# Opening a projection phase with four interleaved value tiles, and wider buffering behind it, in a gated cross-attention block

## What is computed

```python
x = x + jnp.tanh(g_xattn[0]) * xattn(_layernorm(x), ctx, ctx, pos, mask, Wq, Wk, Wv, Wo)
x = x + jnp.tanh(g_ffn[0]) * ffn(_layernorm(x), gate_w, gate_b, w1, b1, w2, b2)
# xattn
q = (query @ Wq).reshape(nb, q_len, H, D).transpose(0, 2, 1, 3)
k = (key @ Wk).reshape(nb, q_len, KVH, D).transpose(0, 2, 1, 3)
v = (value @ Wv).reshape(nb, q_len, KVH, D).transpose(0, 2, 1, 3)
q = q * cos + _rotate_half(q) * sin
k = k * cos + _rotate_half(k) * sin
scores = jnp.einsum('bhqd,bhkd->bhqk', q, k) / jnp.sqrt(jnp.float32(D))
attn = jax.nn.softmax(jnp.where(mask == 0, -1e9, scores), axis=-1)
return jnp.einsum('bhqk,bhkd->bhqd', attn, v).transpose(0, 2, 1, 3).reshape(nb, q_len, H * D) @ Wo
```

## Time and profile before

| | |
|---|---|
| median of 3 runs | 736.51 us (736.07 to 739.14) |
| profiled execution, its own time | 737.81 us |
| its span, first to last instruction | 736.0 us |
| PE busy | 704.6 us, 96% |
| DVE busy | 558.4 us, 76% |
| POOL busy | 402.6 us, 55% |
| ACT busy | 357.0 us, 49% |
| granted TensorE clock, mean | 0.993 |
| moved by DMA | 71.10 MB, 97 GB/s |

### The profile page before, as it was taken

How to read it: one execution, slowest core, us unless ns; L and a number is a source line. 1 busy time by engine, 2 the same in 40 slices (tenths; PEclk the granted TensorE clock), 3 DMA queues, 4 the chain that set the end, 5 groups by cost and what they waited for, 6 DMA issues and landing times.

```text
span 736.0 us, 11337 instructions
## 1 busy us (share of the span) xinstructions
PE 704.6 (96%) x3478; PEld 587.7 (80%) x3478; DVE 558.4 (76%) x924; ACT 357.0 (49%) x955; POOL 402.6 (55%) x340
## 2 busy tenths in 40 slices
PE   5798899899999999999999999999999879999998
PEld 3686688688888888888888888888888766788886
DVE  4977778778878787878888887878787984378832
ACT  5522452455554545454545545454545574872130
POOL 5653524665766666666657566666666541383020
PEclk9999999999999999999999999999999999999999
DMA  8695465432133131212213112222222310240101
GB/s 285 223 288 204 171 216 185 129 101 64 52 87 87 58 87 57 82 61 72 71 36 109 58 56 86 86 57 87 58 77 67 104 69 29 58 115 14 58 1 58
DMA packets 66111, 71.10 MB, mean 97 GB/s; under 512 B 8592, under 2 KB 42384, under 8 KB 66064
## 3 DMA queue, kind: packets, MB, share of 16 engines
q1 hardware_dynamic: 65680, 69.51, 30.1%
q0 software_dynamic: 384, 1.05, 0.4%
HBM read 51.66 MB, written 18.87 MB: 96 GB/s over the span
## 4 chain that ended last, share of the span: by engine, by line
PE 82%; DVE 6%; issue 5%; ACT 3%; POOL 3%; DMA 1%; SPq 0%; POOLq 0%; ACTq 0%; DVEq 0%
PE q L263 34%; PE y L253 28%; PE o L590 5%; PE s L542 5%; PE pt L464 4%; PE s L544 2%; PE o L253 1%; PE pt L253 1%; ACT prob L840 1%; POOL roped L1033 1%; DVE rot L1141 1%; DVE rot L1142 1%; DVE rot L1140 1%; DMA wraw<-in_L_xattn_Wk 1%; POOL scores L1033 1%
## 5 line engine op out<-in xcount | busy, mean ns | idle before, releaser
L263 PE MATMUL q<-xT_hi,big 128*128 128x512 f32 x704 | 235.9, 400 | 0.4 <-issue 0.4
L253 PE MATMUL y<-big,split 128*128 128x512 f32 (+1 forms) x784 | 193.0, 392 | 2.9 <-DVE split L1113 2.9
L253 PEld LDWEIGHTS y<-big,split 128*128 128x128 f32 x784 | 147.9, 189 | 34.5 <-DVE split L1113 3.9
L263 PEld LDWEIGHTS q<-xT_hi,big 128*128 128x128 f32 x704 | 132.2, 188 | 27.3 <-issue 0.6
L263 PE MATMUL q<-xT_lo,big 128*128 128x512 f32 x352 | 136.9, 389 | 0.0
L1060 POOL TENSOR_TENSOR roped<-rot 128x512 f32<-128x512 f32 x59 | 76.4, 1295 | 104.1 <-DVE rot L1142 104.1
L840 ACT ACTIVATE prob<-scores,nmax 128x128 f32<-128x128 f32 x256 | 99.8, 391 | 22.2 <-DVE nmax L1245 22.2
L828 ACT ACTIVATE big<-roped 128x512 fp32r<-128x512 f32 x64 | 40.5, 633 | 142.3 <-POOL roped L1060 137.6
L1076 POOL TENSOR_TENSOR prob<-prob,prec 128x512 f32<-128x512 f32 x64 | 66.6, 1040 | 50.7 <-DVE prec L1259 50.7
L1064 POOL TENSOR_TENSOR big<-roped,big 128x512 fp32r<-128x512 f32 x64 | 82.8, 1294 | 13.4 <-ACT big L828 13.4
L1052 POOL TENSOR_TENSOR big<-wraw,big 128x512 fp32r<-128x512 f32 x64 | 83.2, 1300 | 1.9 <-ACT big L820 1.9
(11 more groups left out here) (170 smaller groups left out, 1141.9 us busy)
## 6 DMA issues: line engine op xcount, KB each, us to landing
k_scratch<-split SPq DMA_DIRECT2D x16, 512.0 KB, 3.5
v_scratch<-split SPq DMA_DIRECT2D x16, 512.0 KB, 3.6
wraw<-in_L_xattn_Wq SPq DMA_DIRECT2D x32, 256.0 KB
wraw<-in_L_xattn_Wo SPq DMA_DIRECT2D x32, 256.0 KB
kv<-k_scratch SPq DMA_DIRECT2D x64, 128.0 KB, 2.5
kv<-v_scratch SPq DMA_DIRECT2D x64, 128.0 KB, 2.8
wraw<-in_L_ffn_w SPq DMA_DIRECT2D x28, 256.0 KB
rows<-ctx_t SPq DMA_DIRECT2D x8, 256.0 KB
```

The source lines that it names most:

```text
L253: mm = pe.matmul(bank_[:, :], stationary(s, c), moving(m, c), start=(c == 0 and n == 0), stop=(c == EC - 1 and n == 2))
L263: mm = pe.matmul(bank_[:, :].rearrange("p (b t) -> p b t", b=BH), weights[s][:, c, h * P:(h + 1) * P], source[m][:, half * BH:(half + 1) * ...
```

## The change

It touches the front and what hangs on its buffers.

- `TILE_ORDER` was `"KKVKVKV" * 4 + "VVVV"` and is `"VVVV" + "KKV" * 8 + "VVVV"`. The first four value tiles run side by side (`first_values`): for each of the first three chunks the hi·hi passes of four batches as soon as both high parts are there, then the four passes with the context's low part, then the four with the weight's; the last chunk goes batch by batch. SP loads Wv before Wk for the first half, and the positions behind the first two pieces.
- All eight context pieces are split before the tiles (it was four, and four among the tiles). The rope gather on POOL waits for the fourth context piece, and the rope tables pass through the banks pt and o.
- Value tiles take four banks, y0, y1, s, and s's second half, in turn.
- Key rotations take `rot` and `prob` in turn (`turned`).
- The scale D^-0.5 becomes D^-0.25 in the rope tables, which both queries and keys pass; L1130's multiply-and-subtract becomes a subtraction (L1159).
- Five staging slots: three of `split`, two of `kv` (`staging`).
- `u_lo` is split in `k_lo` and `v_lo`; layer norms come at tiles 6, 9, 12, 15 (before 9, 11, 13, 16), the first Wq pieces are split at 16 to 19 (before 14 to 17).

```diff
-NST = 3
+NST = 5
-TILE_ORDER = "KKVKVKV" * 4 + "VVVV"
+TILE_ORDER = "VVVV" + "KKV" * 8 + "VVVV"
-LN_AT = (9, 11, 13, 16)
+LN_AT = (6, 9, 12, 15)
+Q_AT = 16
-        rope_bank = [tbank, ybank[1]]
+        rope_bank = [pbank, obank]
+        def value_bank(n):
+            return (ybank + [sbank, tbank])[n % 4] if n < 3 * BH else ybank[n % 2]
+        def bank_user(n):
+            return n - 4 if n < 3 * BH + 2 else n - 2
-            slots = [k % NST for k in range(4 * B - 1)] + [0]
+            slots = [k % NST for k in range(TILES_A)] + [0, 1, 2, 0]
+        def staging(slot):
+            if slot < 3:
+                return split[:, slot, :, :]
+            return kv[:, 2 * (slot - 3):2 * (slot - 2), :, :].rearrange("p n k d -> p n (k d)")
+        def turned(n):
+            return (rot, prob)[n % 2]
...
+            def first_values():
+                def part(c, b, s, m):
+                    return pe.matmul(value_bank(b)[:, :], cT[s][0][:, b, c, :], wb[0][m][:, c, :],
+                                     start=(c == 0 and (s, m) == (0, 0)), stop=(c == EC - 1 and (s, m) == (0, 1)))
+                for c in range(EC - 1):
+                    pe.wait_ge(c_hi, c + 1)
+                    pe.wait_ge(w_hi, c + 1)
+                    for b in range(BH):
+                        part(c, b, 0, 0)
+                    pe.wait_ge(c_lo, c + 1)
+                    for b in range(BH):
+                        part(c, b, 1, 0)
+                    pe.wait_ge(w_lo, c + 1)
+                    for b in range(BH):
+                        part(c, b, 0, 1)
+                pe.wait_ge(c_lo, EC)
+                pe.wait_ge(w_lo, EC)
+                for b in range(BH):
+                    part(EC - 1, b, 0, 0)
+                    part(EC - 1, b, 1, 0)
+                    part(EC - 1, b, 0, 1).then_inc(v_proj, 1)
+            def value_tile(n):
+                pe.wait_ge(v_lo, bank_user(n) + 1)
...
+            pool.wait_ge(c_in[EC - 1], 16)
...
             for m in range(TILES_A):
                 keys, half, k, n = tile_a(m)
                 if keys:
...
+                    elif n == 1:
+                        dve.wait_ge(rope_t, 4)
                     else:
-                        dve.wait_ge(k_roped, n)
+                        dve.wait_ge(k_roped, n - 1)
...
-                    rotate(qbank[n % 2], k // HG, k_rot)
+                    rotate(turned(n), qbank[n % 2], k // HG, k_rot)
-                if m >= 1:
-                    tile_lo(m - 1)
+                if m >= 1 and not tile_a(m - 1)[0]:
+                    value_lo(m - 1)
+                if m >= 1 and tile_a(m - 1)[0]:
+                    key_lo(m - 1)
```

More of the change, by code:

```diff
@@ L48 @@
 VISION = int(P * 0.3)
-SCALE = float(D) ** -0.5
+ROOT_SCALE = float(D) ** -0.25
 MASKED = -2.0 ** 100
@@ L220, in build @@
         for half in range(GH):
-            for m in (Wk, Wv):
+            for m in ((Wv, Wk), (Wk, Wv))[half]:
                 w_chunks += [m[c * P:(c + 1) * P, half * 512:(half + 1) * 512] for c in range(EC)]
@@ L470, in row_transpose @@
                     pe.wait_ge(row_lo, t - 1)
+                else:
+                    pe.wait_ge(rope_ok, 4)
                 transpose4(trans[t % 2], lambda c: rows[:, t % NROW, c * P:(c + 1) * P], row_t)
@@ L481, in _ @@
             pe.wait_ge(ident_ok, 2)
[L483 to L499, removed]
@@ L501, in _ @@
-            for m in range(TILES_A):
-                keys, half, k, n = tile_a(m)
[L503 to L510, removed]
-                if keys:
+            def first_values():
[19 more added lines that the diff above has]
+                    part(EC - 1, b, 0, 1).then_inc(v_proj, 1)
@@ new lines, in value_tile @@
+            def value_tile(n):
+                pe.wait_ge(v_lo, bank_user(n) + 1)
+                project(pe, value_bank(n), lambda s, c: cT[s][n % B // BH][:, n % BH, c, :],
+                        lambda s, c: wb[n // B][s][:, c, :]).then_inc(v_proj, 1)
+            first_values()
+            rope_transpose(0)
+            rope_transpose(1)
+            for m in range(BH, TILES_A):
+                keys, half, k, n = tile_a(m)
+                if keys:
+                    if n == 0:
+                        pe.wait_ge(w_lo, 2 * EC)
+                    if n == HG:
+                        pe.wait_ge(c_lo, PIECES)
+                    if n == B:
+                        pe.wait_ge(w_lo, 3 * EC)
@@ L520, in _ @@
                         pe.wait_ge(c_lo, PIECES)
[L521 to L524, removed]
+                    if n == B:
+                        pe.wait_ge(w_lo, 4 * EC)
+                    value_tile(n)
                 if m >= X_AT:
@@ L539, in unit @@
                         pe.wait_ge(s_sum, i - LAG_S)
+                    else:
+                        pe.wait_ge(v_lo, 3 * BH)
                     for h in range(HG):
@@ L1160, in w_lo_ @@
                 subtract_hi(buf[1][:, c, :], wraw[:, n % NW, :], buf[0][:, c, :], w_lo)
-            for k in range(EC):
+            for k in range(W_DVE):
                 c_lo_(k)
                 w_lo_(k)
-            for n in range(EC, W_DVE):
-                w_lo_(n)
             for m in range(TILES_A):
```

118 lines of the change are left out of this document (57 added, 61 removed).

## The result

The changed kernel takes 732.19 us (median of 5 runs, 730.56 to 733.54) against 736.51: ratio 0.9934, interval 0.991 to 0.9959, so 0.7% faster. The forecast was 723 us, the range 717.5 to 731.5. The direction was right; two thirds of the forecast gain of 13.6 us did not come. The time lies close to two rivals of the prediction, B (731.3) and C (733.4), and neither is what happened: in the profiles the opening won 0.2 us and the rest of the front 5.6, the reverse of B, and in the front the clock fell once, not in every group.

What follows compares the result with a forecast made beforehand. PE bounds the kernel, busy 96% of the span, with 27 of the front's 107.6 us waits or slow matmuls. Gain 5.2 in the opening plus 8.4 behind it, 13.6: 736.5 - 13.6 = 722.9, 723 us; range 717.5 to 731.5.

Steps and rivals of the forecast that it cites:

- B: Rival: only the opening wins, 5.2 us; the rest of the front takes 79 us as before; 731.3 us, chance 0.17.
- C: Rival: small PE waits drop the clock once in each of eight groups, costing 10.4 us; 733.4 us, chance 0.09.
- the opening: Front's start: five tiles and all rope groups done by 23.3 us where it was 28.57, winning 5.2 us.
- the rest of the front: The 23 tiles and 8 row groups up to the units, held by DVE: wins 8.4 us.
- Opening, the matmuls: First four value tiles: PE starts at 5.4 us, twelve slow matmuls to 11.0, all done at 19.2.
- Opening, the gather: POOL's rope gather: starts about 8.3, takes 10.3 us, to 18.6; wanted at 22.6, so hidden, 2 us for landing.
- D: Rival: PE's waits keep the clock at its lower level through the tiles, 5.6 us each; 741 to 788, chance 0.04.
- The groups: DVE's chain per K, K, V group: 7.95 us, plus 1.62 for layer norms in groups 1 to 4.
- A collision with POOL: DVE and POOL both reading two SBUF inputs lengthen one another: 0.6 us in each of four groups, 2.4 in all.
- The value waits: PE's 7.6 us of waits for two value banks in the front go, with four banks.
- Behind the front: From the first query matmul to the end: the same distance as before, 628 us.
- Cover: 0.9 us: Start of the units: DVE's query rotation ends at 101.2, PE needs it at 102.1, so nothing is lost.

Runs made afterwards that it cites:

- norms_first: The changed kernel with the layer norms of tiles 6, 9, 12 and 15 ahead of their group's second key subtraction instead of behind it: 724.84 us.
- gather_free: The changed kernel, but POOL's gather no longer waits for the fourth context piece: 725.49 us.
- two_banks: The changed kernel, but from the fifth value tile on the values use only banks y0 and y1: 731.71 us.
- one_turn: The changed kernel with one rotation buffer, so each rotation waits for POOL's addition of the key before: 736.28 us.
- both: The changed kernel with POOL's gather not waiting for the fourth context piece and the layer norms moved ahead of the second key subtraction: 719.67 us.

## Why the prediction was wrong

*Opening, the matmuls: right.* Start at 5.05 for 5.4; fourth tile done at 18.75 for 19.2; unbroken in between. Twelve matmuls ran at the pitch of the lower level, to 10.4 us, where 11.0 was forecast.

*Opening, the gather: wrong, and this is the step that failed.* "It takes 10.3 us, so to 18.6 ... hidden, with 2 us for the landing." Three terms of it were mis-sized, all one way: the start (9.96 for 8.3), the eight issues (11.7 for 10.3), and above all the landing, 5.4 us for 2. Why the issues took longer is open: the loads ran beside them in the kernel before as well (DMA share 0.98 from 4 to 15 us), and in the other runs of late and free gathers they took from 10.3 to 11.8. The prediction had no row for the landing of an indirect load and took 2 us with no bound; in before, its cover was so wide that nothing showed. The rows were in at 27.1 for 20.6, wanted at 22.6: the cover of 2 us met an error of 6.5. The run without the wait gives the price: 6.7 us in the medians, 6.2 at the start of the units, of which 4.5 is idle time and 1.7 the slow clock behind it. With it gone, the second key tile started at 23.35 for a forecast of 23.3, so the rest of the opening's sum was right. The Trainium skill ("DMA: Bandwidth & Descriptors", "Anatomy of one DMA — SWDGE (gpsimd) path") gives about 2 us plus the bytes by the bandwidth for one DMA issued by this path; here 4.4 (norms_first, 21.03 to 25.47) to 5.4 us were measured with the loads beside it, and the measurement decides.

*The clock: rival C, once in the front.* There the idle of 4.11 us brought the fall, the small ones (0.4 to 1.5 us) none, and in the tile it cost 1.3 us, the size taken. D did not come. But the prediction read more safety out of the rows than the trace of the kernel before holds. It looked at the front alone, where waits of 1.38 and 0.69 us left the clock up. At 605 us of the same trace the clock falls although the 16 us ahead of it hold no wait longer than 0.75 us, only seven of 0.27 to 0.75 (the tile of 4.60 us above). And the changed kernel has a second fall, at 136 to 140 us, behind a wait of 2.53 us in the seam.

*The groups: right.* From 52.11 to 61.86 and to 71.64, 9.75 and 9.78 us per group with layer norms, for 7.95 + 1.62 = 9.57; DVE's wait 1.90 for 1.91; PE's waits 0.5 to 1.5 us. A collision with POOL cost 0.36 us (1.05 for 0.69), not 0.6, and came in three groups, not four. That the norms are the removable part of it is shown by norms_first. The prediction stated the order "the key is still subtracted right after its rotation" as a wait that remains, which it did. Without the gather's wait, DVE began the last group at 90.30 us (gather_free), for 90.6 in the sum: the chain was right to 0.3 us. What it had wrong is the step behind it, that PE waits for DVE there. From 72.78 us on PE ran without a break to the units.

*The value waits: right that they go, wrong why.* The prediction gave them to the four banks; two_banks has none of them with two.

*Behind the front: wrong by 2.4 us in the seam*, or 2.9 with the gather repaired, where the prediction had nothing; 0.9 and 1.3 in the span, because the profiles of these two kernels lack the late fall. "Cover: 0.9 us" looked at PE and DVE alone. In the changed kernel PE waits there 1.41 and 2.53 us for POOL (before: 2.00), and ACT up to 3.6 us for a Wq piece (before: 1.1). SP's queue was not followed in the prediction: the Wq piece stands in it behind key/value loads that wait for the last stores' landing. That this is the cause is likely, as said above, not shown.

*The sum.* By the profile the changed kernel's span ended 8.7 us behind the forecast (731.1 for 94.0 + 628.4): 6.2 are the gather, 1.6 the rest of the front (95.6 for 94.0, mostly PE's wait of 1.5 us for ACT's normed rows, which the chain had left out), 2.4 the seam, less 1.5 for the late fall that this execution was spared. In the medians it is 9.2. Without the gather's wait the forecast would have been missed by 2.5 us and the time would have lain in its range; part of that closeness is luck, since the seam's loss and the missing fall have opposite signs.

## What to carry to other kernels

When a change delays a transfer, cost its issue and its landing apart, from rows; if the trace has only landings that were hidden, the landing is unknown and belongs in the range, with the idle time and the slow clock behind it. An engine's fixed wait is a place to put independent work: a few lines moved ahead of DVE's wait gave 7.3 us on top of a redesign that had given 4.3. When two runs are compared by the length of a stretch, look at the clock in it too: one fall of 1.5 us in one profile and not in the other hid most of a loss here. When one change removes a wait in two ways (more banks, another order), undo them one by one before keeping the costly one.

## What the runs showed of the hardware

- Eight indirect loads of POOL took 10.3 us (before) to 11.8 us (gather_free) to issue, each time beside context and weight loads that kept the DMA engines at a share near 1; where PE waited for them, their last rows were in 4.4 (norms_first) to 5.4 us (changed) after the last issue.
- The clock fell behind idles of TensorE of 2.87 and 3.36 us (before), 4.11 and 2.53 us (changed) and 1.89 us (one_turn, at 130 us), and at 605 us of the kernel before with no wait above 0.75 us in the 16 us ahead. It stayed at 1.00 behind one of 2.80 us (two_banks, 26 to 30 us) and behind 2.54 us (both, 122 to 126 us). So the length of the last idle does not decide it alone; what does was not tested. Each fall showed as 3 to 5 us at 0.50 and cost 1.3 to 1.6 us where PE had no wait behind it to take it up. In the seam it cost less: from 135.44 to 141.83 the changed kernel took 6.39 us with the fall, from 122.27 to 128.54 both took 6.27 without it, since short waits went instead.
- The clock goes with the spread of 3 us between executions of the changed kernel: the fastest (730.56) had a mean granted clock of 0.997, the slowest (733.54) 0.991.
- A DVE subtraction of two SBUF operands took 1.05 us beside a POOL subtraction, 0.69 without; in the earlier trace rows it was 1.78.
